# GpSimd's landing wait ahead of the row fetches: every fourth chunk in place of every second

## The chip, the cores and the metric

The kernel runs on one core of one Trainium2 chip. The metric is the device time of the whole launch in microseconds (us). The engines are called by their short names: PE is TensorE, DVE is VectorE, ACT is ScalarE, POOL is GpSimd and SP is SyncE. Each has its own instruction stream, and they meet only in semaphores.

## What is computed

The reference is a network of four layers over x, which has 2 x 1024 tokens of width 256, in float32. Each layer adds to x the outcome of a small conditioning network followed by a feed-forward network. Only two of them matter here: the feed-forward part of the first layer, and the conditioning part of the third.

```
# first layer, feed-forward: 8 heads, K = 8, 4096 experts of width 256
xn = rmsnorm(x) ; q = xn @ w_q.T
s1, i1 = top_k(sim1, 8) ; s2, i2 = top_k(sim2, 8)
fs, pk = top_k(s1[..., :, None] + s2[..., None, :], 8)
fi = ids of the experts picked                       # 64 a token
hidden = gelu(einsum('btd,bthkd->bthk', xn, expert_down[fi])) * relu(fs)
x = x + einsum('bthk,bthkd->btd', hidden, expert_up[fi])
...
# third layer, conditioning: for each of 2 picked skills and a shared one
out += weight * (gelu(x @ gate) * (x @ up)) @ down   # width 256 -> 1024 -> 256
```

## The kernel before

The program is a row of stages (`begin`, `peer`, `lora`, `skills`, `quant_ffn`, `attend`, `tail`). The tokens are worked in four blocks of 512. For the first three blocks, the experts of the first layer are computed densely on PE in `peer`. The fourth block goes another way. Its 512 tokens are four tiles of 128, each token has 64 experts, and the rows of these experts (down and up side by side, 512 floats) are fetched from a table in HBM by indirect DMAs. One indirect DMA brings one expert's row for each of 128 tokens, 256 KB. Eight of them (`RROWS`) are a **chunk**, and there are 32 chunks (`NCH`), numbered n = 0 to 31. The fetches of chunks 0 and 1 are issued in `lora`, all others in `skills`.

The chunks go round a **ring of three buffers** (`NRING`), in the rows of the profile `layer_qw` (n = 0, 3, 6, ...), `layer_w` (n = 1, 4, ...) and `four_ring` (n = 2, 5, ...). Each buffer has its own semaphore, `row_load[0..2]` (in the order `all_row_load0` to `2`), which rises by 16 for each DMA that has landed. A fetch is issued by `fetch_rows` (L814 to L820).

In `skills` this work of the fourth block runs beside the third layer's skill networks of all blocks. These are a plan of 96 steps j (four blocks, three networks, eight slices of the inner width). A step is three groups of four matmul instructions on PE: gate into `skills_ps_g` and up into `skills_ps_u` (L1499), and, for step j-2, down into `skills_acc` (L1444). ACT applies gelu (L1515), and DVE multiplies (`hidden`, L1169). Each pair of steps carries one chunk. In the even step, DVE waits until the chunk has landed and takes eight dot products (`product`, L1227, rows at L1235); in the odd step ACT applies gelu to the dots (`hidden_rows`, L1521), and DVE weighs the chunk's up rows into the sum (`gather`, L1238, rows at L1241 and L1247), a chain in which each instruction waits for the semaphore of the one before it (`vstep`; the mark `used` is its value after a chunk). In chunks 0 to 13, DVE also works through 14 parts of the expert choice for the last two tiles (`pick`, L1172; its many small instructions nearly all raise `vstep`). PE's step 65 (`TURN3`, L1459) waits for the mark of chunk 31, since there the fourth block's sum is turned and joins the rest.

What sets the order of POOL is written by hand (L1411 to L1419). Ahead of chunk n it waits for the experts' ids of a new tile, then for `used` of chunk n - 3, which frees the buffer, and then, in every second chunk, until the chunk just issued, n - 1, has landed:

```
                if n >= NRING:
                    pool.wait_ge(vstep, marks["used", n - NRING])
                if n % 2 == 0:
                    pool.wait_ge(g.row_load[(n - 1) % NRING], 16 * RROWS * ((n - 1) // NRING + 1))
                fetch_rows(pool, g, rows[n % NRING], n)
```

No data depends on the last of these waits: the reader of a chunk, `product`, waits for the landing itself.

## Time and profile before

| what | us |
|---|---|
| median of 3 runs | 1633.42 (1632.73 to 1634.76) |
| the profiled execution's own time | 1636.18 |
| its span in the profile | 1634.5 |
| `skills`, from its first matmul to the next stage | about 684 to 1247 |
| of it, the stretch with row fetches | 684 to 1068 |

The profile is of one execution, 0.17% above the median; times in rows are counted from the start of its span. 1.7 us of the execution lie outside the span.

### The profile page before, as it was taken

The page shows a single profiled execution, that of the slowest core. Times are in us where ns is not written, and L with a number is a line of the kernel's source. Part 1 is how long each engine was busy: PE and PEld are TensorE (multiplying, and loading weights), DVE is VectorE, ACT ScalarE, POOL GpSimd, SP SyncE. Part 2 cuts the span into 40 slices and gives each one's busy share as a digit, 9 for nine tenths or more (in the row PEclk, how much of TensorE's full clock was granted, in tenths as well). Part 3 has the DMA queues.
Part 4 walks back from the last instruction along what each step waited for, and adds up shares of the span by engine and source line. Part 5 has one row for each costly group of instructions (what it writes and reads, how often), then busy time and mean ns, then how long its engine had stood idle before and what let it go on. Part 6 is the DMA issues. An engine that isn't in the chain of part 4 may idle for free. (4 is left out here: it accounts for less than half of the span.)

```text
span 1634.5 us, 26893 instructions
## 1 busy us (share of the span) xinstructions
PE 1510.3 (92%) x10648; PEld 922.2 (56%) x10648; DVE 1072.4 (66%) x3225; ACT 450.6 (28%) x695; POOL 461.6 (28%) x392
## 2 busy tenths in 40 slices
PE   7999789999999999898979998889999999999882
PEld 3447678888888887443434443344444457544761
DVE  1639889696868746478879667634783398613735
ACT  2333111111111100133323333221112476712442
POOL 0002322323222512356665666600000000000363
PEclk9999789999999999999989999999999999999985
DMA  8910000000000013485556765520142027100235
GB/s 354 240 17 1 2 2 8 2 8 3 9 3 9 3 34 122 139 273 181 170 174 194 251 216 173 174 116 0 51 156 65 0 78 235 36 7 0 75 132 103
DMA packets 91025, 155.93 MB, mean 95 GB/s; under 512 B 42524, under 2 KB 56981, under 8 KB 88853
## 3 DMA queue, kind: packets, MB, share of 16 engines
q1 hardware_dynamic: 68884, 82.91, 15.8%
q0 software_dynamic: 22016, 71.32, 14.7%
q8 instruction: 84, 1.38, 0.3%
q14 instruction: 41, 0.33, 0.1%
HBM read 141.62 MB, written 16.78 MB: 97 GB/s over the span
## 5 line engine op out<-in xcount | busy, mean ns | idle before, releaser
L521 PE MATMUL peer_ps_h<-all_x,layer_down 128*128 128x256 f32 x768 | 182.5, 392 | 0.0
L659 POOL TENSOR_TENSOR peer_bm<-peer_bm,peer_slots 128x512 f32<-128x512 f32 x36 | 109.0, 3028 | 244.8 <-DVE peer_bm L755 244.8
L521 PEld LDWEIGHTS peer_ps_h<-all_x,layer_down 128*128 128x128 f32 x768 | 145.9, 194 | 22.5 <-issue 2.1
L560 PE MATMUL peer_ps_o<-peer_hg,layer_up 128*128 128x256 f32 x640 | 142.3, 380 | 0.2 <-DVE peer_hg L787 0.2
L604 ACT ACTIVATE peer_hg<-peer_ps_h 128x512 f32<-128x512 f32 x96 | 57.3, 597 | 273.6 <-PE peer_ps_h L521 273.6
L560 PEld LDWEIGHTS peer_ps_o<-peer_hg,layer_up 128*128 128x128 f32 x640 | 120.5, 190 | 20.2 <-issue 3.3
L1499 PE MATMUL skills_ps_u<-all_x,skills_w 128*128 128x512 f32 x256 | 122.4, 601 | 8.1 <-DVE skills_hid L1169 4.1
L1444 PE MATMUL skills_acc<-skills_hid,skills_w 128*128 128x512 f32 x256 | 121.9, 600 | 7.0 <-issue 4.5
L1499 PE MATMUL skills_ps_g<-all_x,skills_w 128*128 128x512 f32 x256 | 123.0, 603 | 0.0
L1515 ACT ACTIVATE skills_act_g<-skills_ps_g 128x512 f32<-128x512 f32 x83 | 49.1, 597 | 234.7 <-PE skills_ps_g L1499 185.5
L819 POOL DMA_INDIRECT layer_qw<-expert_rows,all_route x88 | 88.1, 1002 | 52.1 <-issue 24.6
L819 POOL DMA_INDIRECT layer_w<-expert_rows,all_route x88 | 87.3, 992 | 51.2 <-issue 26.4
L787 DVE TENSOR_TENSOR peer_hg<-peer_ps_w,peer_hg 128x1024 f32<-128x1024 f32 x48 | 58.7, 1223 | 61.7 <-PE peer_ps_w L536 61.6
L819 POOL DMA_INDIRECT four_ring<-expert_rows,all_route x80 | 78.9, 986 | 42.7 <-issue 23.0
L659 POOL TENSOR_TENSOR all_route<-all_route,peer_slots 128x512 f32<-128x512 f32 x12 | 36.3, 3028 | 187.5 <-DVE all_route L755 187.5
L1499 PEld LDWEIGHTS skills_ps_u<-all_x,skills_w 128*128 128x128 f32 x256 | 48.9, 192 | 71.5 <-issue 64.7
L1444 PEld LDWEIGHTS skills_acc<-skills_hid,skills_w 128*128 128x128 f32 x256 | 48.9, 192 | 71.3 <-issue 66.6
L1749 PE MATMUL quant_ps_m<-layers_y,layer_qw 128*128 128x512 f32 x192 | 85.8, 602 | 2.0 <-DVE layers_y L1656 2.0
L536 PE MATMUL peer_ps_w<-peer_bm,peer_am 64*64 64x32 f32 x4608 | 77.9, 224 | 10.1 <-DVE peer_hg L787 8.4
L536 PEld LDWEIGHTS peer_ps_w<-peer_bm,peer_am 64*64 64x64 f32 x4608 | 73.9, 140 | 22.2 <-issue 22.2
L1499 PEld LDWEIGHTS skills_ps_g<-all_x,skills_w 128*128 128x128 f32 x256 | 49.5, 195 | 61.4 <-issue 61.4
L757 DVE TENSOR_TENSOR peer_am<-all_iota_a,peer_slots 128x2048 f32<-128x2048 f32 x36 | 82.3, 2285 | 0.0
(457 smaller groups left out, 2621.7 us busy)
## 6 DMA issues: line engine op xcount, KB each, us to landing
four_ring<-in_l_w SPq DMA_DIRECT2D x8, 1024.0 KB, 4.8
quant_w<-in_l_w SPq DMA_DIRECT2D x32, 256.0 KB, 4.3
all_early<-in_l_w SPq DMA_DIRECT2D x26, 256.0 KB, 3.6
skills_w<-in_skills SPq DMA_DIRECT2D x16, 384.0 KB
layer_down<-in_down SPq DMA_DIRECT2D x1, 4096.0 KB, 26.3
layer_up<-in_up SPq DMA_DIRECT2D x1, 4096.0 KB, 35.2
expert_rows<-in_up SPq DMA_DIRECT2D x1, 4096.0 KB, 41.1
four_skill<-in_skills SPq DMA_DIRECT2D x1, 3072.0 KB
```

Of the source, the lines that this page charges most:

```text
L521: mm = pe.matmul(ps_h[group % 2][:, r, :], down[:, c, j * P:(j + 1) * P], g.x[:, c, bass.ds(i * PB, PB)], start=(c == 0), stop=(c == C - 1))
L536: mm = pe.matmul(ps_w[of, z, m, :], am[c % RING][token, m, of], bm[c % RING][token, m, :], start=True, stop=True)
L560: mm = pe.matmul(ps_o[:, c, :], up[:, j, c * P:(c + 1) * P], hg[half][:, j, :], start=(j == 0), stop=(j == NJ - 1))
L604: act.activation(hg[half][:, 2 * group:2 * group + 2, :], ps_h[group % 2][:], ACT.Gelu).then_inc(gelu_done, 1)
L659: pool.tensor_tensor(bm[c % RING][:], bm[c % RING][:], slots[half][:, 2, c * PAIRS:(c + 1) * PAIRS].unsqueeze(2).to_broadcast([P, PAIRS, WJ]),
L757: dve.tensor_tensor(am[c % RING][:], g.iota_a[:].unsqueeze(1).to_broadcast([P, PAIRS, P]), slots[half][:, 0, col].unsqueeze(2).to_broadcas ...
L787: dve.tensor_tensor(acts, ps_w[:].rearrange("p z m j -> p z j m"), acts, ALU.mult).then_inc(p_done, 1)
L819: pool.indirect_dma_start(to[:, k, :], None, g.table, bass.IndirectOffsetOnAxis(ap=g.eid[:, n // per, at:at + 1], axis=0)).then_inc(g.row_ ...
L1444: mm = pe.matmul(acc[c][:], w_down[s][:, m, c * P:(c + 1) * P], hid[j % 4][:], start=(s == 0 and m == 0), stop=(s == 2 and m == M2 - 1))
L1499: mm = pe.matmul(to[:], weight[:, c, m * P:(m + 1) * P], g.x[:, c, q * BLK:(q + 1) * BLK], start=(c == 0), stop=(c == C - 1))
L1515: act.activation(act_g[bank[j]][:], ps_g[bank[j]][:], ACT.Gelu_apprx_tanh).then_inc(gelu_done, 1)
L1749: mm = pe.matmul(ps_m[n % n_ring][:], wt[z][:, c, m * P:(m + 1) * P], g.y[:, c, q * BLK:(q + 1) * BLK], start=(c == 0), stop=(c == C - 1))
```

## The change

POOL waits for the landing of the chunk before only ahead of every fourth chunk. In the order of instructions nothing else moves on any engine.

```diff
@@ skills, block.gpsimd
                 if n >= NRING:
                     pool.wait_ge(vstep, marks["used", n - NRING])
-                if n % 2 == 0:
+                if n % 4 == 0:
                     pool.wait_ge(g.row_load[(n - 1) % NRING], 16 * RROWS * ((n - 1) // NRING + 1))
                 fetch_rows(pool, g, rows[n % NRING], n)
```

The wait goes ahead of n = 2, 6, 10, 14, 18, 22, 26 and 30, and stays ahead of n = 4, 8, 12, 16, 20, 24 and 28.

On POOL, from chunk 5 to chunk 8 of the kernel before (the first row of a chunk bears its waits; `skills_vstep` is the mark `used`, `all_row_load...` the landing):

```order
L819 DMA four_ring<-expert_rows,all_route 128x512 [waits skills_vstep]
L819 DMA four_ring<-expert_rows,all_route 128x512 x7
L819 DMA layer_qw<-expert_rows,all_route 128x512 [waits all_row_load2,skills_vstep]
L819 DMA layer_qw<-expert_rows,all_route 128x512 x7
L819 DMA layer_w<-expert_rows,all_route 128x512 [waits skills_vstep]
L819 DMA layer_w<-expert_rows,all_route 128x512 x7
L819 DMA four_ring<-expert_rows,all_route 128x512 [waits all_row_load1,skills_vstep]
```

The same place in the changed kernel:

```order
L819 DMA four_ring<-expert_rows,all_route 128x512 [waits skills_vstep]
L819 DMA four_ring<-expert_rows,all_route 128x512 x7
L819 DMA layer_qw<-expert_rows,all_route 128x512 [waits skills_vstep]
L819 DMA layer_qw<-expert_rows,all_route 128x512 x7
L819 DMA layer_w<-expert_rows,all_route 128x512 [waits skills_vstep]
L819 DMA layer_w<-expert_rows,all_route 128x512 x7
L819 DMA four_ring<-expert_rows,all_route 128x512 [waits all_row_load1,skills_vstep]
```

Chunk 6, in `layer_qw`, no longer waits for the landing of chunk 5; chunk 8 still waits for that of chunk 7.

Of the kernel before, what the change touches and what calls it, by code (L numbers as in the profile page):

```python
# [813 lines left out]
def fetch_rows(pool, g, to, n):  # L814

    per = SLOTS // RROWS
    for k in range(RROWS):
        at = n % per * RROWS + k
        pool.indirect_dma_start(to[:, k, :], None, g.table, bass.IndirectOffsetOnAxis(ap=g.eid[:, n // per, at:at + 1], axis=0)  # L819
                                ).then_inc(g.row_load[n % NRING], 16)  # L820
# [252 lines left out]
def skills(nc, a, g):  # L1073

    with Stage(nc, "skills") as st:
# [65 lines left out]
        for name, times in (("xt_ready", 1), ("xt_kept", C), ("t_ready", 1), ("t_done", C), ("h_ready", 1), ("hs_done", 1),  # L1141
                            ("l_ready", 1), ("ex_done", 1), ("wide_done", 1), ("w_ready", 1), ("hw_done", 1), ("o_ready", C), ("x_done", C)):
            after[name] = sum(n for _, n in after.values()) + times, times
        after = {name: n for name, (n, _) in after.items()}
        block = st.block()
        plan = [(q, s, m) for q in range(NBLK) for s in range(3) for m in range(M2)]
# [260 lines left out]
        @block.gpsimd  # L1407
        def _(pool):
            for t in (gate3[:], wide3):
                pool.memset(t, -1.0 if t is not wide3 else 1.0).then_inc(presets, 1)  # L1410
            for n in range(NRING - 1, NCH):  # L1411
                t, k0 = n // (SLOTS // RROWS), n % (SLOTS // RROWS) * RROWS
                if t >= 2 and k0 == 0:
                    pool.wait_ge(vstep, marks["eid", t])
                if n >= NRING:
                    pool.wait_ge(vstep, marks["used", n - NRING])
                if n % 2 == 0:
                    pool.wait_ge(g.row_load[(n - 1) % NRING], 16 * RROWS * ((n - 1) // NRING + 1))
                fetch_rows(pool, g, rows[n % NRING], n)  # L1419
            pool.memset(warm[:, 0:1], 0.0).then_inc(presets, 1)  # L1420
            pool.wait_ge(presets, 3)
            pool.partition_all_reduce(warm[:, 1:2], warm[:, 0:1], P, bass.bass_isa.ReduceOp.max).then_inc(presets, 1)
            pool.wait_ge(presets, 4)
# [1197 lines left out]
```

## Rows read from the trace of the kernel before

**Rows 1.** The page, part 1: busy time, share of the span, instructions.

```profile
PE 1510.3 (92%) x10648; PEld 922.2 (56%) x10648; DVE 1072.4 (66%) x3225; ACT 450.6 (28%) x695; POOL 461.6 (28%) x392
```

**Rows 2.** Busy time by stretch: both halves of the fetches.

```profile
core 0: us, PE busy (x) PEld busy (x) DVE busy (x) ACT busy (x) POOL busy (x), PEclk, DMA share, GB/s
684.00:865.00 181.00, 166.50 (x383) 73.06 (x382) 145.27 (x558) 61.50 (x78) 112.23 (x113) 0.96 0.65 205
865.00:1068.00 203.00, 181.97 (x415) 78.05 (x413) 147.42 (x484) 69.55 (x90) 127.41 (x130) 0.99 0.64 197
```

**Rows 3.** PE in order of time: the gate groups of two successive steps.

```profile
923.98 1.88 PE L1499 MATMUL skills_ps_g<-all_x,skills_w 128*128 128x512 f32 x4
...
929.13 1.88 PE L1499 MATMUL skills_ps_g<-all_x,skills_w 128*128 128x512 f32 x4
```

**Rows 4.** PE's waits, 684 to 1070: total, times, longest.

```profile
PE skills_ps_u L1499 <- remote: 9.6, 1, 9.6
PE skills_acc L1444 <- issue: 8.8, 5, 2.3
PE skills_ps_g L1464 <- DVE layers_y L1247: 5.7, 1, 5.7
PE skills_ps_u L1499 <- DVE skills_hid L1169: 4.1, 1, 4.1
...
```

**Rows 5.** POOL in order of time: first DMA of chunks 6, 10, 14, 18, 22, 26, 30.

```profile
737.99 0.94 POOL L819 DMA_INDIRECT layer_qw<-expert_rows,all_route  x1 [3.49 <-DMA four_ring<-expert_rows,all_route]
...
788.61 0.94 POOL L819 DMA_INDIRECT layer_w<-expert_rows,all_route  x1 [3.42 <-DVE skills_s L1180]
...
839.89 0.94 POOL L819 DMA_INDIRECT four_ring<-expert_rows,all_route  x1 [7.30 <-DVE layers_y L1247]
...
892.50 0.94 POOL L819 DMA_INDIRECT layer_qw<-expert_rows,all_route  x1 [4.73 <-DMA four_ring<-expert_rows,all_route]
...
940.12 0.94 POOL L819 DMA_INDIRECT layer_w<-expert_rows,all_route  x1 [3.47 <-DVE layers_y L1247]
...
989.68 0.94 POOL L819 DMA_INDIRECT four_ring<-expert_rows,all_route  x1 [3.57 <-DMA layer_w<-expert_rows,all_route]
...
1037.14 0.94 POOL L819 DMA_INDIRECT layer_qw<-expert_rows,all_route  x1 [3.37 <-DMA four_ring<-expert_rows,all_route]
```

**Rows 6.** POOL in order of time: the last DMA of chunk 31.

```profile
1056.41 1.06 POOL L819 DMA_INDIRECT layer_w<-expert_rows,all_route  x1 [0.30 <-issue]
```

**Rows 7.** DVE in order of time: gathers of chunks 22 and 23, product and gather of 31.

```profile
957.26 2.05 DVE L1247 SCALAR_TENSOR_TENSOR layers_y<-layer_w,skills_wacts,layers_y 128x256 f32<-128x256 f32 x4
...
962.94 0.48 DVE L1247 SCALAR_TENSOR_TENSOR layers_y<-layer_w,skills_wacts,layers_y 128x256 f32<-128x256 f32 x1 [0.21 <-DVE layers_y L1247]
...
968.09 4.17 DVE L1247 SCALAR_TENSOR_TENSOR layers_y<-four_ring,skills_wacts,layers_y 128x256 f32<-128x256 f32 x8
...
1060.18 0.42 DVE L1235 SCALAR_TENSOR_TENSOR layer_w<-layer_w 128x256 f32<-128x256 f32 x1 [0.94 <-DMA layer_w<-expert_rows,all_route]
...
1063.80 4.13 DVE L1247 SCALAR_TENSOR_TENSOR layers_y<-layer_w,skills_wacts,layers_y 128x256 f32<-128x256 f32 x8
```

**Rows 8.** All engines in order of time: the stall at 824 to 836.

```profile
824.19 0.22 DVE L1198 FIND_INDEX8 skills_p<-skills_f,skills_mask 128x8 uint32<-128x64 f32 x1
...
829.77 0.23 DVE L1198 FIND_INDEX8 skills_p<-skills_f,skills_mask 128x8 uint32<-128x64 f32 x1 [1.20 <-issue]
...
835.49 3.78 PE L1499 MATMUL skills_ps_u<-all_x,four_skill 128*128 128x512 f32 x4 [9.64 <-remote]
```

**Rows 9.** Instructions by line: duration min/median/max in ns.

```profile
L819 POOL DMA_INDIRECT layer_qw<-expert_rows,all_route x88: 940/946/1381, 640.6 to 1046.1; - x88
L1247 DVE SCALAR_TENSOR_TENSOR layers_y<-layer_w,skills_wacts,layers_y x84: 483/485/522, 705.4 to 1065.9; 128x256 f32<-128x256 f32 x84
```

**Rows 10.** POOL's first DMA of chunk 15, DVE's gather of chunk 13.

```profile
851.31 0.94 POOL L819 DMA_INDIRECT layer_qw<-expert_rows,all_route  x1 [1.34 <-DVE layers_y L1247]
...
858.04 4.14 DVE L1247 SCALAR_TENSOR_TENSOR layers_y<-layer_w,skills_wacts,layers_y 128x256 f32<-128x256 f32 x8
```

## The prediction

> **What bounds the kernel now.** The page says of the whole span that PE is busy for 92% [rows 1]. The change touches one stretch, so the next view is the busy time by stretch [rows 2]. In the two halves of the row fetches PE is busy for 166.50 of 181 us and 181.97 of 203 us, at a granted clock of 0.96 and 0.99. PE is therefore nearly the bound and not quite: 14.5 and 21.0 us, 35.5 us in all, are idle there. PE's own waits name where [rows 4]: 9.6 us in one piece, 8.8 in five, 5.7 at the end, 4.1 in one more, and smaller ones.
>
> Next come the paces of the two engines that could set the rhythm of a chunk. PE, undisturbed, begins a step every 929.13 - 923.98 = 5.15 us [rows 3]; a chunk takes two steps, 10.3 us. POOL issues a DMA in 0.94 us or a little more and leaves 0.30 us before the next [rows 6, 9], so a chunk of eight costs it 8 x (0.946 + 0.30) = 10.0 us at the median duration and a few tenths more in fact. The two are almost equal as long as POOL does nothing else. But POOL does wait: the first DMAs of chunks 6, 18, 26 and 30 stand behind 3.4 to 4.7 us of idle time that a landing ends, and chunks 10 and 22 behind 3.4 and 3.5 us [rows 5]. The last two are put down to DVE, but DVE's instruction named there has nothing to do with the ring at chunk 10 (it is a piece of the expert choice), and the length is that of a landing; I read them as landings too. From the first DMA of chunk 22 at 940.12 to that of chunk 30 at 1037.14, eight chunks take 97.0 us, 12.1 us each. That is what PE's 10.3 us have to follow, so in the second half POOL is the bound.
>
> That the end of the stretch hangs on POOL is seen at the end itself. Chunk 31's last DMA is issued by 1057.47 [rows 6]. DVE, after a wait of 0.94 us for this landing, starts its product at 1060.18 and ends the gather at 1063.80 + 4.13 = 1067.93 [rows 7]. PE waited 5.7 us for just that [rows 4]. Everything behind it in the stage starts from there.
>
> **The change, part by part.** It removes eight waits and adds no instruction.
>
> *Chunk 2.* The landing of chunk 1 lies a whole stage boundary back (its buffer was fetched in `lora`). Nothing waits here; the price is 0, also if the cover is gone, since nothing is left of it.
>
> *Chunks 6, 10, 18, 22, 26, 30.* What goes is the idle time of POOL beyond the 0.30 us that it leaves between two DMAs anyway: 3.49 + 3.42 + 4.73 + 3.47 + 3.57 + 3.37 = 22.05 us, less 6 x 0.30 = 1.8, is 20.25 us [rows 5]. All of it comes off the chain above only if POOL doesn't meet its other wait, for the chunk three back. Chunk 23's gather ends at 968.09 + 4.17 = 972.26 [rows 7], and its buffer is refilled by chunk 26 at 989.68 [rows 5]: 17.4 us to spare, of which the landing wait was 3.6. Two or three removed waits add up to 10 us before the kept ones are reckoned, and the others in the chain (landing, product, gather) begin earlier with the fetch. I count the 20.25 us in full.
>
> *Chunk 14.* Here POOL idled 7.30 us until DVE's gather freed the buffer [rows 5]. The landing would have been over about 3.4 us after the issue, before that. Removing the wait gives 0 if DVE is no earlier, and at most 3.4 - 0.3 = 3.1 us if DVE comes forward with it. I take 0, since DVE was held there by the stall of [rows 8].
>
> *Cover on PE.* A gain of 20.25 us is smaller than the 35.5 us that PE idles. PE's 10.3 us a chunk is then the next limit but isn't reached.
>
> *What comes back.* The trace shows an effect that a landing wait seems to undo. The gather is a chain in which each instruction waits for the one before. At its normal speed eight instructions take 4.13 us (chunk 31, when POOL has stopped issuing) or 4.17 (chunk 23, when POOL has just paused). Chunk 22's gather, while POOL was issuing the last of sixteen DMAs in a row, runs from 957.26 to 962.94 + 0.48 = 963.42, 6.16 us [rows 7]. The instructions are no longer, 483 to 522 ns all of them [rows 9]; the gaps between them are. So semaphore steps get slow late in an unbroken run of DMAs. A short pause is enough against it: chunk 15 was issued behind one of 1.34 us, and the gather at 858.04 beside it took 4.14 us [rows 10]. Before, every second chunk falls in such a late part, 15 of the 30 here. With a pause in every fourth chunk three of four do, 22 of 30, so seven more. Each costs from 0 (hidden behind the wait for a landing) to 6.16 - 4.15 = 2.0 us; between ends of like weight I take the middle, 1.0 us: 7.0 us, with ends of 0 and 14.
>
> *Sum.* -20.25 + 7.0 = -13.25 us. The profiled execution took 1636.18 us, so 1622.9 for its like; against the median of 1633.42 the forecast is **1620.2 us**, 0.8% less. The bounds of the terms give -23.4 (chunk 14 gained too, nothing back) to -6.3 (14 us back): 1610.0 to 1627.2.
>
> How long a landing lasts can be set beside a rule. The Trainium skill, page "DMA: Bandwidth & Descriptors", section on the anatomy of one DMA, gives 2.0 us plus the bytes by 436 GB/s for a DMA of this path, which is 2.6 us for 256 KB. Estimated by that page, the six removed waits would be 6 x (2.6 - 0.3) = 13.8 us in place of 20.25. The rows show 3.4 us and more, and the measurement decides.
>
> **The rivals.**
>
> *The slow steps become stalls (slower).* At 824 to 836 the same effect was far worse. DVE was in a part of the expert choice, with many small instructions that each raise a semaphore; a FIND_INDEX8 that had followed at once now came 1.20 us late, and PE then stood still for 9.64 us [rows 8]. POOL was in the second chunk after a pause, as above. The expert choice has 14 parts, in chunks 0 to 13, and with pauses half as often about half as many more parts fall into late stretches. Price: 9.64 us for each further stall. Three of them give 28.9 - 20.25 = +8.7 us, **1642.1 us**; from 20.25 / 9.64 = 2.1 stalls on it decides. For it: the stall exists, and a run of 32 DMAs is longer than any in this trace. Against it: one such stall in 15 late chunks, a second of 4.1 us at most [rows 4]; and a late DVE makes POOL wait for its buffer, which is a pause in itself. The Trainium skill, page "GPSIMD Engine Reference", key points, says that GpSimd shares its SBUF interfaces with VectorE and contends with instructions of two SBUF inputs, which the gather's are. By it, more issuing beside DVE would lengthen DVE's instructions; the durations in [rows 9] don't show that for DVE, though single issues of POOL reach 1381 ns.
>
> *Nothing comes back (much faster).* If the slow steps hide behind landings, or are the profiler's own load and absent from the timed runs, the whole 20.25 us stay: **1613.2 us**, down to 1610.0. For it: POOL's pace isn't slowed by the effect, and POOL is what is followed.
>
> *The other wait takes over (no change).* POOL comes to each chunk 3 us earlier and waits there for `used`, as at chunk 14. Then **1633.4 us**. Against it: the 17.4 us to spare at chunk 26; it needs DVE to be late in most groups.
>
> **How the numbers follow.** The forecast (1616 to 1628) has 0.33, nothing back 0.22, stalls 0.32, the other wait 0.13. A change within 0.2%, 3.3 us, is about what a measurement of this kernel can't tell from none. So faster is 0.33 + 0.22 = 0.55, the same 0.13, slower 0.32. The range goes from 1609, just under the bound of nothing back, to 1642, which is three stalls and leaves out about half of that rival, 0.16, and little below. The forecast's own range is 1610 to 1627, by its bounds.
>
> **What would show it.** In the trace after, POOL's first DMAs of chunks 6, 10, 18, 22, 26 and 30 stand behind 0.30 us, and those of 8, 12, 16, ... behind 3.4 us or more. From chunk 22 to 30 the eight chunks take 97.0 less two removed waits of 3.2, some 90.6 us. Chunk 31's last DMA comes about 13 to 20 us before 1056.41, and PE's idle time in the stretch falls from 35.5 to about 22. The gathers in the third and fourth chunk of a run take 5 to 6 us in place of 4.15. The prediction is wrong if PE shows new waits of several us while POOL issues without a break, or if POOL's idle time moves from landings to DVE.

## The result and the profile after

The change made the kernel slower: 1659.4 us in the median of 4 runs (1647.98 to 1662.04), beside 1634.09 for the kernel before in the same measurement, a ratio of 1.0134 with a 95% interval of 1.0103 to 1.0164. The profiled execution took 1659.96 us against 1636.18, 23.8 more.

The page, part 1, of the changed kernel: the same instructions and nearly the same busy time as in [rows 1].

```profile
PE 1513.7 (91%) x10648; PEld 924.4 (56%) x10648; DVE 1074.0 (65%) x3225; ACT 450.9 (27%) x695; POOL 461.3 (28%) x392
```

The busy time by stretch, beside [rows 2] (start:end, length, then busy time of each engine, granted clock, DMA share, GB/s):

```profile
684.00:865.00 181.00, 157.38 (x357) 68.79 (x356) 136.22 (x529) 57.42 (x73) 104.59 (x107) 0.94 0.63 194
865.00:1068.00 203.00, 170.63 (x381) 74.41 (x380) 133.63 (x431) 63.89 (x82) 125.67 (x127) 0.91 0.65 196
```

PE idles for 23.6 + 32.4 = 56.0 us where it idled for 35.5, at a granted clock of 0.94 and 0.91 in place of 0.96 and 0.99. PE's waits, 684 to 1095 (total, times, longest), beside [rows 4]:

```profile
PE skills_acc L1444 <- DVE skills_hid L1169: 16.1, 2, 12.0
PE skills_ps_u L1499 <- DVE skills_hid L1169: 15.4, 3, 9.0
PE skills_acc L1444 <- remote: 14.5, 1, 14.5
PE skills_ps_u L1499 <- remote: 8.1, 1, 8.1
```

Where one wait of over 5 us in a step stood before, there are five (9.0, 6.2, 8.1, 12.0 and 14.5 us), and one of 4.1. Step 65 doesn't wait at all now (5.7 us before): PE is later than the chunks.

The first instruction of step 65, the place where the fourth block's sum is turned, starts at 1067.99 before and at 1094.29 in the changed kernel, 26.3 us later. PE in order of time before:

```profile
1067.99 1.11 PE L1464 MATMUL skills_ps_g<-all_ident,layers_y 128*128 128x128 f32 x4 [5.65 <-DVE layers_y L1247]
```

The busy time up to this place, before and then in the changed kernel:

```profile
684.00:1067.99 383.99, 348.46 (x796) 151.10 (x795) 292.68 (x1041) 131.05 (x168) 239.65 (x243) 0.98 0.65 201
684.00:1094.29 410.29, 354.30 (x795) 154.62 (x794) 295.15 (x1041) 131.34 (x168) 239.10 (x243) 0.93 0.62 188
```

So 20.5 us of the 26.3 are idle time of PE, and 5.8 are the same matmuls taking longer at a lower granted clock. Behind this place the changed kernel needs 565.7 us where the one before needs 568.2. That makes 20.5 + 5.8 - 2.5 = 23.8 us, the whole difference.

POOL in order of time, chunks 6, 10, 18, 22, 26 and 30, then the last DMA of chunk 31, beside [rows 5, 6]:

```profile
736.62 0.95 POOL L819 DMA_INDIRECT layer_qw<-expert_rows,all_route  x1 [0.30 <-issue]
...
791.59 0.95 POOL L819 DMA_INDIRECT layer_w<-expert_rows,all_route  x1 [0.30 <-issue]
...
899.46 1.02 POOL L819 DMA_INDIRECT layer_qw<-expert_rows,all_route  x1 [0.30 <-DVE layers_y L1247]
...
1052.40 0.94 POOL L819 DMA_INDIRECT layer_qw<-expert_rows,all_route  x1 [0.30 <-issue]
...
1077.96 1.16 POOL L819 DMA_INDIRECT layer_w<-expert_rows,all_route  x1 [0.30 <-issue]
```

The removed waits are gone (chunks 22 and 26, not shown, also start behind 0.30 us), and yet the last issue ends at 1079.12, 21.6 us later than in [rows 6]. What ended POOL's idle time ahead of L819, 684 to 1130, in the kernel before (total, times):

```profile
  issue: 69.7, 223
  DVE layers_y L1247: 24.1, 6
  DMA four_ring<-expert_rows,all_route: 16.4, 4
  DMA layer_w<-expert_rows,all_route: 7.0, 2
  DMA layer_qw<-expert_rows,all_route: 6.8, 2
  DVE skills_s L1180: 3.4, 1
  DVE skills_i L1184: 3.4, 1
  DVE skills_i L1187: 3.4, 1
```

And in the changed kernel:

```profile
  issue: 71.2, 225
  DVE layers_y L1247: 68.7, 10
  DVE skills_wacts L1241: 5.3, 1
  DVE skills_i L1187: 4.1, 1
  DMA layer_w<-expert_rows,all_route: 3.5, 1
  DMA layer_qw<-expert_rows,all_route: 3.4, 1
  DVE skills_f L1195: 0.3, 1
```

Waits put down to landings fell from 30.2 to 6.9 us, and those put down to DVE rose from 34.3 to 78.4. Not all of DVE's are waits for `used`: before, four of them, at chunks 4, 10, 12 and 22, are 3.37 to 3.47 us long, the length of a landing. Read as landings, as the prediction did for two of them, they leave 20.6 us of waits for `used` before and 43.9 us for landings; in the changed kernel one of 4.08 us, at chunk 12, can be either. So the waits for `used` rose by 54 to 58 us and those for landings fell by 33 to 37. The balance, +20.8 us either way, is nearly all of POOL's 21.6.

How DVE got late is seen in the worst stall. DVE in order of time, while POOL issues the third and fourth of four chunks without a pause (product of chunk 25, `hidden`, then the first instruction of the gather):

```profile
1005.90 0.42 DVE L1235 SCALAR_TENSOR_TENSOR layer_w<-layer_w 128x256 f32<-128x256 f32 x1
...
1007.14 0.42 DVE L1235 SCALAR_TENSOR_TENSOR layer_w<-layer_w 128x256 f32<-128x256 f32 x1 [0.81 <-issue]
...
1008.57 0.42 DVE L1235 SCALAR_TENSOR_TENSOR layer_w<-layer_w 128x256 f32<-128x256 f32 x1 [1.00 <-issue]
...
1010.70 0.42 DVE L1235 SCALAR_TENSOR_TENSOR layer_w<-layer_w 128x256 f32<-128x256 f32 x1 [1.34 <-issue]
...
1013.52 0.42 DVE L1235 SCALAR_TENSOR_TENSOR layer_w<-layer_w 128x256 f32<-128x256 f32 x1 [1.31 <-issue]
...
1016.32 0.75 DVE L1169 SCALAR_TENSOR_TENSOR skills_hid<-skills_ps_u,all_pair_w,skills_act_g 128x512 f32<-128x512 f32 x1 [2.01 <-issue]
1024.30 0.17 DVE L1241 TENSOR_TENSOR skills_wacts<-skills_acts,all_route 128x8 f32<-128x8 f32 x1 [7.23 <-ACT skills_acts L1521]
```

The other engines at the same place: POOL's last DMA before the pause, ACT's gelu of the dots, PE's down matmuls of step 51, and POOL's first DMA behind the pause.

```profile
1021.41 0.95 POOL L819 DMA_INDIRECT layer_qw<-expert_rows,all_route  x1 [0.30 <-issue]
...
1024.06 0.21 ACT L1521 ACTIVATE skills_acts<-skills_dots 128x8 f32<-128x8 f32 x1 [21.33 <-remote]
...
1026.17 3.78 PE L1444 MATMUL skills_acc<-skills_hid,four_skill 128*128 128x512 f32 x4 [14.51 <-remote]
...
1031.25 0.94 POOL L819 DMA_INDIRECT layer_w<-expert_rows,all_route  x1 [8.89 <-DVE layers_y L1247]
```

The instructions keep their 0.42 us, but the last four dot products start 1.24, 1.43, 2.13 and 2.82 us after the one before in place of 0.35. By the kernel's code all waits of a product stand ahead of its first dot product; behind it nothing is waited for, and each dot product only raises `mul_done`. So not only what waits for an update is late here, DVE itself is held. The `hidden` at 1016.32 is that of step 51 and ended at 1017.07; PE, which waits for nothing else there, began at 1026.17. ACT, DVE and PE all move again 1.7 to 3.8 us after POOL's last issue has ended (1022.36). The profile brackets an instruction's execution; the Trainium skill, page "Perfetto Trace Analysis", section "Per-engine timelines", says that the propagation of a semaphore update comes behind it and is in no row. The trace agrees, and shows more: beside the rows of instructions it records when semaphores rose, and for the one that PE waits for here it has 1026.12, 9.05 us behind the end of `hidden` and 0.05 ahead of PE's start. (Such records are not complete, 75 for this semaphore's 96 updates.) Where nothing is late the whole way is short: before, DVE's last gather ended at 1067.93 [rows 7] and PE started at 1067.99. The matmul group behind the stall takes 3.78 us where 1.88 is normal [rows 3]: PE had idled for 14.5 us, and from 1026.20 to 1029.90 its granted clock is 0.50, which is 1.2 GHz in place of 2.4.

### The profile page after: what moved, and what is told of

Same layout as the page of the kernel before. It is cut to its first block and busy times, and to the rows that moved or that the text cites. A ratio compares the mean times of both kernels' runs of the same rounds, so it can differ in the third digit from the quotient of the medians.

```text
span 1658.2 us, 26886 instructions
## 1 busy us (share of the span) xinstructions
PE 1513.7 (91%) x10648; PEld 924.4 (56%) x10648; DVE 1074.0 (65%) x3225; ACT 450.9 (27%) x695; POOL 461.3 (28%) x392
## 5 line engine op out<-in xcount | busy, mean ns | idle before, releaser
L1499 PE MATMUL skills_ps_u<-all_x,skills_w 128*128 128x512 f32 x256 | 123.8, 607 | 15.4 <-DVE skills_hid L1169 15.4
L819 POOL DMA_INDIRECT layer_w<-expert_rows,all_route x88 | 86.7, 986 | 68.6 <-issue 26.4
L819 POOL DMA_INDIRECT layer_qw<-expert_rows,all_route x88 | 87.1, 990 | 43.9 <-issue 26.3
L819 POOL DMA_INDIRECT four_ring<-expert_rows,all_route x80 | 79.9, 999 | 55.6 <-DVE layers_y L1247 29.4
## 6 DMA issues: line engine op xcount, KB each, us to landing
layer_down<-in_down SPq DMA_DIRECT2D x1, 4096.0 KB, 25.7
```

Of the source, the lines that this page charges most:

```text
L819: pool.indirect_dma_start(to[:, k, :], None, g.table, bass.IndirectOffsetOnAxis(ap=g.eid[:, n // per, at:at + 1], axis=0)).then_inc(g.row_ ...
L1499: mm = pe.matmul(to[:], weight[:, c, m * P:(m + 1) * P], g.x[:, c, q * BLK:(q + 1) * BLK], start=(c == 0), stop=(c == C - 1))
```

## The experiments

**Theory A**: where POOL issues indirect DMAs about 1.25 us apart without a pause, the semaphore updates of the other engines arrive later and later; steps stretch and PE stalls, and a pause on POOL lets the late updates through. The rivals are named in the expectations. A ratio below is to the kernel before, timed beside it, with the 95% interval. The edits are shown against the kernel before where the text doesn't name the changed one, and shortened (`...`).

**No landing wait at all, and one ahead of every chunk.**

```diff
-                if n % 2 == 0:
-                    pool.wait_ge(g.row_load[(n - 1) % NRING], ...)
```

> The landing wait is taken out at every chunk; only the waits for the ids and for the used buffer are left. Theory A, unbroken issuing: where POOL issues indirect DMAs without a pause, semaphore updates of the other engines arrive late, and PE stalls by 4 to 15 us at a time. Without any landing wait the unbroken rows of DMAs are at least as long as in the changed kernel, so the time is no better than its 1659.4: 1655 to 1690, with at least 55 us of waits of PE at L1444 and L1499 in the stretch 684:1095, and waits of POOL for the used buffers. Rival B, the changed kernel loses only by where its few remaining waits fall against the buffers' release: with none left POOL is only bound by its issues, and the time is at or under 1620. Rival C, bandwidth of the transfers: the same bytes in the same time as in the changed kernel, 1650 to 1665.

Measured: 1647.23 us, 1.0098 (1.0060 to 1.0136). POOL's idle time ahead of L819 in this kernel:

```profile
  DVE layers_y L1247: 65.3, 12
```

Rival B falls: the time isn't at or under 1620, and with no landing wait left, 65.3 us of waits for `used` stand in their place. Theory A's range, 1655 to 1690, is missed too; PE's waits at its two lines come to 37 us, not 55 or more, with one of 13.5. By its median this kernel is better than the changed one, though their intervals overlap. So fewer landing waits are not simply worse. The waits for `used` are pauses too; that it matters where they fall is my reading, and no run tests it.

```diff
-                if n % 2 == 0:
+                if n > NRING - 1:
```

> The landing wait stands ahead of every chunk. POOL's chunk then takes about 9.9 us of issue and 3.4 us of pause, 13.4 us in place of a mean of 11.7 us, so the fetches of 30 chunks end some 45 us later, about 1102. Theory A: rows of only 8 DMAs never slow the semaphores, so PE has no stall over 4 us at L1444 or L1499 ahead of its step 65, which now waits long for chunk 31; the time is 1634 plus 45 less up to 25 of stalls given back: 1654 to 1680. Rival D, the stalls come from DVE's own load (the expert choice of chunks 0 to 13 and the dots) and not from POOL: stalls of 4 to 10 us stay in the stretch 684:865, as many as in the kernel before, and the time is 1675 to 1685.

Measured: 1680.63 us, 1.0293 (1.0257 to 1.0328). PE's waits, 684 to 1095:

```profile
PE skills_acc L1444 <- DVE skills_hid L1169: 42.5, 15, 4.6
```

The stalls are gone, in the stretch of the expert choice too (no wait over 3.5 us there): what is left is 15 waits of 2.8 us on average, 4.6 at most, where POOL is the bound. Rival D falls by the trace, though the time lies in its range and just above theory A's 1680. The 25 us that I gave back to theory A were not there to be had: POOL's last issue ends at 1103.27, 45.8 us after that of the kernel before, and the profiled time is 45.8 us longer.

**A pause of other work where the landing wait was removed.** The edit is against the changed kernel, without the lines that set up the semaphore `idle` and its count. `wide3` already holds ones, so the writes change nothing.

```diff
                 if n % 4 == 0:
                     pool.wait_ge(g.row_load[(n - 1) % NRING], ...)
+                if n % 4 == 2:
+                    for _ in range(6):
+                        pool.memset(wide3, 1.0).then_inc(idle, 1)
+                        idled += 1
+                        pool.wait_ge(idle, idled)
```

> The changed kernel, and at each place where the landing wait was removed POOL does some 3 us of other work, six small writes that nothing reads, so there is a pause in issuing but no wait for a landing. Theory A: the pause alone brings back the kernel before, 1628 to 1642, and PE's waits at L1444 and L1499 in 684:1095 fall from 55.8 us to about 35. Rival B, it is the wait for the landing or the meeting with the buffers' release that matters: the time stays within 5 us of 1659, or over it by the 21 us of added work, 1655 to 1682.

Measured: 1632.38 us, 0.9996 (0.9979 to 1.0014), the kernel before again. POOL in order of time at chunk 30:

```profile
1028.61 3.26 POOL L1424 MEMSET all_early<- 128x472 f32 x6
1032.14 1.06 POOL L819 DMA_INDIRECT layer_qw<-expert_rows,all_route  x1 [0.27 <-POOL all_early L1424]
```

PE's waits, 684 to 1095:

```profile
PE skills_acc L1452 <- issue: 10.3, 6, 2.3
PE skills_ps_u L1507 <- DVE skills_hid L1170: 6.0, 4, 2.4
PE skills_acc L1452 <- DVE skills_hid L1170: 5.8, 7, 1.2
```

No stall over 5 us is left; all waits at the two lines come to 25.7 us, fewer than the 35 expected. It is the pause in issuing, not the landing, that the kernel before lives on.

**Half the bytes, and half the pieces, in each DMA**, both in the changed kernel.

```diff
-        pool.indirect_dma_start(to[:, k, :], None, g.table, ...)
+        pool.indirect_dma_start(to[:, k, 0:D], None, g.table.rearrange('e (two d) -> (e two) d', two=2), ...)
...
-                    row, by, to = rows[n % NRING][:, k, D:2 * D], ...
+                    row, by, to = rows[n % NRING][:, k, 0:D], ...
```

> The changed kernel with the same number of indirect DMAs, each of half the bytes: 128 pieces of 1 KB, from half rows of the table (the fetched rows are not the experts' rows, and the weighted sum takes the first half in place of the up rows, so this part of the output is not the reference's). Theory A, the count of DMAs issued without a pause does it: 1645 to 1665, with stalls of PE over 8 us. Rival C, bytes on the DMA engines or in HBM: the stalls go, and with POOL's 20 us of removed waits in hand the time is 1612 to 1630.

Measured: 1654.67 us, 1.0116 (1.0058 to 1.0175). The transfers moved 123 and 115 GB/s in the two halves in place of 194 and 196, and the time is still far above rival C's 1612 to 1630: rival C falls. Theory A's time is right, but not its stalls of over 8 us: PE's longest wait is 6.4 us, and all of them come to 37.5 us in place of 55.8. Halving the bytes may thus have eased the stalls; the interval overlaps that of the changed kernel, so the time doesn't settle it.

```diff
-    per = SLOTS // RROWS
+    per, some = SLOTS // RROWS, P if n < NRING else P // 2
...
-        pool.indirect_dma_start(to[:, k, :], ..., ap=g.eid[:, n // per, ...]
+        pool.indirect_dma_start(to[0:some, k, :], ..., ap=g.eid[0:some, n // per, ...]
```

> The changed kernel, and from chunk 3 on each indirect DMA fetches its rows for 64 of the 128 tokens (the other half of the buffers keeps old rows, so this part of the output is not the reference's): half the pieces and half the bytes a DMA, and the same number of DMAs. Theory Q, what piles up is the work of one DMA's pieces (its 128 descriptors and what they bring with them): the stalls of PE go, and since the waits of POOL are short as well the time is 1600 to 1625. Theory N, each issue counts whatever it carries: stalls over 8 us and 1640 to 1665; if the issue also gets shorter, the DMAs come closer together and it is no better for it.

Measured: 1655.78 us, 1.0144 (1.0113 to 1.0175). POOL in order of time:

```profile
997.77 0.90 POOL L819 DMA_INDIRECT four_ring<-expert_rows,all_route  x1 [0.30 <-issue]
```

PE's longest wait:

```profile
PE skills_acc L1444 <- ACT layers_y L1528: 12.4, 1, 12.4
```

With half the pieces an issue is hardly shorter, 0.90 us for 0.95, and a stall of 12.4 us is there: theory Q falls, and theory N's range holds. The loss in time stays whether an issue carries all or half of the bytes or pieces. One thing that comes with each DMA was never varied: however small it is, it raises its `row_load` by 16 when it lands. So these runs can't tell the issue on POOL from the updates at the landing.

**Fewer semaphore updates on the side that suffers**: only the last dot product of a chunk raises `mul_done`, in the changed kernel and in the kernel before.

```diff
-                                             accum_out=dots[...]).then_inc(mul_done, 1)
+                                                  accum_out=dots[...])
+                op.then_inc(mul_done, 1)
...
-                act.wait_ge(mul_done, RROWS * (n + 1))
+                act.wait_ge(mul_done, n + 1)
```

> The changed kernel with fewer semaphore updates on DVE: only the last of the eight dot products of a chunk raises mul_done, and ACT waits for one a chunk. DVE then sends 17 updates a chunk less 7, of some 19 in a pair of steps. Theory F, the load that suffers is the number of DVE's updates, each held for some 1.3 us behind the issues of POOL: with a third of them gone the stalls shrink by a third or more, 1640 to 1652, and PE's waits at L1444 and L1499 in 684:1095 are 40 us or less. Theory A alone (any update that meets an unbroken row of issues is late, the chain of gather and hidden most of all): 1652 to 1663, waits of PE over 45 us.

> The kernel before, the landing wait at every second chunk, with the same fewer semaphore updates of the dot products. Theory F: the kernel before has 35.5 us of such waits of PE, of which a third goes, 1620 to 1629. Theory A alone: 1630 to 1636, no difference.

Measured: 1665.39 us, 1.0196 (1.0154 to 1.0238), and 1630.08 us, 0.9996 (0.9979 to 1.0012). Theory F falls in both: with fewer of these updates nothing gets faster. The first is even 2 us above what theory A gave. Its trace also limits theory A. In it the first seven dot products of a chunk raise no semaphore, and behind the first none waits for one. DVE in order of time, the end of the sixth dot product of chunk 8 and the start of the seventh:

```profile
789.64 0.08 DVE L1235 DVE_READ_ACCUMULATOR four_ring<-four_ring,layer_qw 128x1 f32 x1 [0.99 <-issue]
790.34 0.42 DVE L1235 SCALAR_TENSOR_TENSOR four_ring<-four_ring,layer_qw 128x256 f32<-128x256 f32 x1 [0.61 <-issue]
```

They are late all the same, by 0.99 and 0.61 us. What POOL's issues hold back is therefore not semaphore updates alone.

**How long a pause, and how spread.** No landing waits in any of these, only small writes: `memset` of `wide3` (three of them, in a block ahead of a chunk) or of `gate3` or a part of `wide3` (one, ahead of each DMA). Shown is the smallest write, ahead of each DMA; the new last argument of `fetch_rows` picks one of the chunk's eight DMAs. The expectations behind it are, in order, those of three writes at every second chunk, the small write ahead of each DMA, three writes at every chunk, the small write ahead of every second DMA, the wider write, the widest, the small write ahead of three DMAs in four, and the one ahead of each again.

```diff
-                if n % 2 == 0:
-                    pool.wait_ge(g.row_load[(n - 1) % NRING], ...)
-                fetch_rows(pool, g, rows[n % NRING], n)
+                for k in range(RROWS):
+                    pool.memset(gate3[:], -1.0).then_inc(idle, 1)
+                    idled += 1
+                    pool.wait_ge(idle, idled)
+                    fetch_rows(pool, g, rows[n % NRING], n, [k])
```

> No landing waits; at every second chunk POOL does three small writes that nothing reads, a pause of about 1.8 us between two rows of 16 DMAs, in place of 3.5 us. Theory A in the form that any pause lets the late updates through: the half pause does as well as the whole, and half of the 20 us on POOL is gained where POOL was the bound, 1620 to 1633. Theory A in the form that a pause has to be as long as what has piled up (about 3 us for 16 DMAs): the backlog grows, 1640 to 1660, with stalls of PE over 6 us.

> No landing waits; the same sum of pauses as before, but spread, one small write of 0.12 us with its semaphore ahead of every DMA, which sets the DMAs some 1.45 us apart in place of 1.26. Theory A as a pile that grows with the unbroken row (a break of 3 us needed): the row is never broken for long, 1645 to 1670 with stalls over 6 us. Theory R, what counts is the mean rate of issues: as the kernel before or better, 1622 to 1636, with no stall over 6 us.

> No landing waits; a pause of three small writes, about 1.9 us, ahead of every chunk: the same sum of pauses as in the run with six of them at every second chunk, in rows of 8 DMAs in place of 16. Theory R, what counts is the mean spacing of the DMAs over some ten to twenty of them (1.26 us unbroken, 1.47 with these pauses): as the kernel before or a little better, since less piles up within a row, 1620 to 1632, no stall of PE over 6 us. Theory A as first put (only a break of some 3 us clears the pile, and this one is the same 1.9 us that failed at every second chunk): 1640 to 1665 with stalls of 7 us and more.

> The small write ahead of every second DMA only: a mean spacing of 1.31 us against 1.36 with one ahead of each and 1.26 with none. Theory R with a pile that grows with what is missing to about 1.4 us: between the two, 1628 to 1645, with several stalls over 6 us. Theory T, what helps is only that a row is broken at all, by however little: as with one ahead of each, 1618 to 1627.

> One write of 118 elements a partition, about 0.22 us, ahead of each DMA, a spacing of about 1.44 us. POOL then needs 346 us for the issues of 30 chunks, and the last comes at about 1045 to 1050 if it never waits, as with the smaller write, where 17 us of waits stood between. Theory R: the last stalls of PE go, and the time is 1615 to 1626. If spacing has nothing to do with it and the smaller write helped by chance of order, stalls over 6 us stay and the time is 1630 or more.

> One write of 236 elements a partition, about 0.35 us, ahead of each DMA, a spacing of about 1.57 us, 377 us for 240 DMAs: the last is issued at about 1070 to 1075, some 15 to 20 us after that of the kernel before, and PE's step 65 waits for chunk 31. Theory R: no stalls at L1444 and L1499 besides those for chunks that land late, and 1640 to 1655 since POOL is now the bound. A time at or under 1625 would say that POOL's own rate never was.

> No landing waits, the small write of 0.14 us ahead of three of every four DMAs: a mean spacing of 1.34 us, between 1.31 (1648.7) and 1.36 (1622.1). Theory R puts it between the two, 1625 to 1640. A time at 1617 to 1622 would say that the best spacing is a little under 1.36.

> The kernel with the small write ahead of each DMA once more, in more rounds, since it was faster than the kernel before: 1615 to 1626, a ratio of 0.992 to 0.997 to the kernel before.

POOL in order of time, with the smallest write ahead of each DMA:

```profile
944.26 0.95 POOL L819 DMA_INDIRECT four_ring<-expert_rows,all_route  x1 [0.27 <-POOL skills_gate L1421]
945.21 0.14 POOL L1421 MEMSET skills_gate<- 128x32 f32 x1
945.62 0.95 POOL L819 DMA_INDIRECT four_ring<-expert_rows,all_route  x1 [0.27 <-POOL skills_gate L1421]
```

With the widest:

```profile
950.24 0.95 POOL L819 DMA_INDIRECT four_ring<-expert_rows,all_route  x1 [0.27 <-POOL all_early L1421]
...
951.77 0.98 POOL L819 DMA_INDIRECT four_ring<-expert_rows,all_route  x1 [0.27 <-POOL all_early L1421]
```

The spacing in the table is that of issues of 0.95 us with no wait between (1.25 bare, 1.36 and 1.53 by these rows), with the pauses spread over their row of DMAs (three writes take 1.6 us more than the usual 0.3 between two issues, and 16 x 1.25 + 1.6, by 16, is 1.35). The fourth column is the longest of PE's waits at its two lines, the fifth the end of POOL's last issue, both of the profiled execution, whose own time is the last.

| POOL | mean spacing | ratio (95%) | longest stall | last issue ends | profiled time |
|---|---|---|---|---|---|
| changed kernel | 1.25 in rows of up to 32 | 1.0134 (1.0103 to 1.0164) | 14.5 | 1079.12 | 1659.96 |
| no landing wait, no write | 1.25 | 1.0098 (1.0060 to 1.0136) | 13.5 | 1063.38 | 1643.98 |
| write ahead of every second DMA | 1.31 | 1.0098 (1.0061 to 1.0136) | 12.4 | 1062.64 | 1647.29 |
| write ahead of three in four | 1.33 | 0.9974 (0.9951 to 0.9997) | 12.2 | 1059.52 | 1633.73 |
| 3 writes at every second chunk | 1.35 | 1.0076 (1.0036 to 1.0117) | 8.2 | 1062.38 | 1645.46 |
| write ahead of each | 1.36 | 0.9946 (0.9927 to 0.9966) | 7.9 | 1045.33 | 1625.10 |
| the same again | 1.36 | 0.9961 (0.9947 to 0.9975) | 4.2 | 1043.01 | 1621.41 |
| wider write ahead of each | 1.44 | 0.9984 (0.9969 to 0.9998) | 3.9 | 1049.64 | 1629.98 |
| 3 writes at every chunk | 1.45 | 0.9989 (0.9976 to 1.0002) | 3.6 | 1050.64 | 1630.74 |
| kernel before | 1.45 | 1 | 9.6 | 1057.47 | 1636.18 |
| widest write ahead of each | 1.53 | 1.0108 (1.0090 to 1.0126) | 4.2 | 1062.97 | 1643.11 |

The medians, from the top: 1659.4, 1647.23, 1648.65, 1628.49, 1645.83, 1622.07, 1624.71, 1629.19, 1630.99 and, at the end, 1649.47 us. The edits with writes have no landing wait, so their measure is the second row. Two things compete. Up to 1.35 us there are stalls of 8 to 14 us, and POOL waits for a late DVE. At 1.36 they are fewer (7.9 us at most in one execution, 4.2 in the other), and from 1.44 on, with evenly set or short rows, no stall is over 4.2 us, but each further 0.1 us on 240 issues delays the last by up to 24 us. The kernel before has bare rows of 16 DMAs and one stall of 9.6 us; its two near twins above, with the work pause and with fewer updates, have none over 5. The best spacing tried is 1.36, with 1.33 within its interval.

The form of theory A in which only a break of 3 us helps falls (the spread write has none), and so does rival T (a write ahead of every second DMA is not enough). A pause of half the length at every second chunk failed as its second form said. Theory R says that the mean spacing decides. It is the best account of these runs, and five of its seven ranges in this series held, but it isn't the whole: 1.33 us set evenly gives 0.9974, and 1.35 in bare rows of 16 gives 1.0076, with intervals that don't meet. How the pauses are spread counts too. Theory R also missed in three places. The small write ahead of each DMA was to have no stall over 6 us, and had one of 7.9; its time is at the very edge of the range. The wider write was expected at 1615 to 1626 and came to 1629.19, since with the last stalls gone there was nothing left to win and POOL was the bound. The write ahead of every second DMA came to 1648.65, above 1628 to 1645, no better than no write at all.

**The faster version** is the one with the small write ahead of each DMA: 0.54% in one measurement and 0.39% in another below the kernel before, and 1.9 and 1.7% below the changed one (0.9946 / 1.0134 = 0.981, 0.9961 / 1.0134 = 0.983). Its busy time by stretch:

```profile
684.00:865.00 181.00, 173.00 (x400) 75.96 (x401) 150.80 (x578) 65.37 (x83) 134.80 (x235) 0.98 0.68 210
865.00:1068.00 203.00, 187.59 (x427) 82.53 (x426) 143.81 (x467) 67.52 (x87) 141.70 (x249) 0.96 0.68 215
```

PE idles for 8.0 + 15.4 = 23.4 us, against 35.5 before and 56.0 in the changed kernel.

## Why the prediction was wrong

*What bounds the kernel* was right for the kernel before. In eleven of the seventeen profiled executions the time is the end of POOL's last issue plus 578.4 to 581.1 us (1636.18 - 1057.47 = 578.7 before, 1659.96 - 1079.12 = 580.8 after). Of the other six, five lie above, at 582.3 to 593.7, and one below at 574.2; the version with fewer updates in the changed kernel, at 593.7, has PE wait until 1078.18 in a stall of 9.5 us, when POOL had ended at 1073.32. In the changed kernel the last issue tells the time but doesn't set it: step 65 waits for nothing there, and POOL and PE are late by the same stalls.

*The removed waits, 20.25 us.* They went as written: chunks 6, 10, 18, 22, 26 and 30 start behind 0.30 us, chunk 14 behind a wait for `used`. The step that failed is "I count the 20.25 us in full", with its reason, 17.4 us to spare at chunk 26. This slack was that of a DVE in time. With DVE late it was used up: POOL waited for `used` 7.6 us on average in nine waits of over 4 us that the gather ended, where the kernel before had three (6.14, 5.35 and 7.30 us, at chunks 3, 8 and 14).

*What comes back, 7.0 us.* This is the term that was mis-sized, and it was priced in the wrong place: on the gather, by 1.0 us a chunk, at seven more chunks. The gathers didn't get slower. Against an undisturbed 4.13 us (3.61 for the four that begin a tile, with seven such instructions) the 32 gathers took 9.4 us too long before and 3.4 in the changed kernel, and those of over 0.3 us too much fell from ten to two. So this term measured -6.0 us where +7.0 was forecast, and the sign that I gave, gathers of 5 to 6 us in the third and fourth chunk of each row, didn't come: the two long ones take 5.33 and 4.86 us, all others 4.21 at most. What came back was the stalls: 20.5 us more of idle PE and 5.8 us of slower matmuls up to step 65. On POOL it shows as 54 to 58 us more of waits for `used`, against 33 to 37 us less of waits for landings. The lateness strikes the product, the expert choice, the gelu and `hidden`, grows along the row of DMAs and ends in a stall.

*"A short pause is enough against it"* was a misreading as well. The pause of 1.34 us at chunk 15 came one chunk behind one of 7.30 us at chunk 14 [rows 5, 10], so the gather there proves nothing; three writes, a pause of 1.9 us, at every second chunk left stalls of 8.2 us.

*The rivals.* "The slow steps become stalls" is what happened, at a price near the one given (6.2 to 14.5 us, 10.0 on average, against 9.64) and with four more stalls in place of three. It would have given 4 x 9.64 - 20.25 = +18.3, and +23.8 was measured; I broke it off at three. "The other wait takes over" was its other half: POOL's time moved to `used`, not in place of the stalls but through them. My argument that a late DVE makes POOL wait, "which is a pause in itself", was right about the relief (1.7 to 3.8 us after the last issue all engines move) and wrong about the price: such a pause lasts 7.6 us on average and up to 10.6, a landing wait 3.4.

*The Trainium skill*, page "GPSIMD Engine Reference", key points, speaks of contention of GpSimd and VectorE for their shared SBUF interfaces. By it DVE's instructions would be longer. In the changed kernel those at L1247 last 483 to 548 ns with a median of 485, as in [rows 9], so the trace doesn't show it in durations. That such contention delays the start of DVE's instructions no run rules out; the 9.05 us between the end of `hidden` and its update it would not explain.

*The 3.4 us of a landing wait*, which the prediction set beside 2.6 us by a rule, are not the landing alone. Before, at 12 of the 14 landing waits from chunk 4 on, POOL's sequencer saw the semaphore full 2.60 to 2.85 us after the end of its last issue, and without a wait for `used` the next DMA started 0.70 us after that. The first part is close to the rule's 2.6 us; the 0.70 us were missing in the estimate of 13.8 us, not in the 20.25 us, which were read from rows.

*The range* ended at 1642 because the stalls were capped at three. Nothing in the trace gave that cap: no row of more than 16 DMAs without a pause was in it.

## What to carry to other kernels

A wait that no data needs may be the pacing of something shared; before removing it, look at what the other engines' steps do late in the longest stretch without such a wait, and don't extrapolate that by a mean per step: price the worst stall, not the slow step. Where one engine issues DMAs back to back, try a little work between the issues: here 0.11 us more per issue beat both a long pause and none, by 0.4 to 0.5% of the kernel before. When a stretch hangs on one queue, follow the end of that queue's last issue; it told the time of most versions here within 2 us. Then look whether the next engine waits for it at all: in the changed kernel it didn't.

## What the runs showed of the hardware

Indirect DMAs issued 1.25 us apart by POOL, by the dozen, make semaphore updates between the other engines late, 9.05 us in the worst case seen closely (`hidden` ended at 1017.07, its update is recorded at 1026.12), while the duration of instructions stays. They also delay the start of DVE's instructions, by up to 1.3 us each, and by up to 0.99 us where these neither wait for a semaphore nor raise one. A pause of 3.3 us of other work every 16 DMAs or so undoes the stalls. At a spacing of 1.36 us they are fewer (7.9 and 4.2 us at most in two executions), at 1.44 none is over 3.9. Halving the bytes or the pieces of a DMA leaves the loss in time, and so does raising `mul_done` once a chunk in place of eight times.

What is shared stays open. The 16 updates that each landing makes were never varied, so they can't be told from the issues. Nor can the load of the recording: every timed run was recorded by the profiler too, and that instructions without any semaphore are late as well would fit a load of records of instructions. No run tests it.
